# Loading half of x's rows through a second DMA queue in a LoRA kernel

## The reference

```python
B_sel = B[adapter_ids]          # (64, 16, 1024)
A_sel = A[adapter_ids]          # (64, 1024, 16)
Bx  = jnp.einsum('bni,bri->bnr', x, B_sel)
out = jnp.einsum('bnr,bor->bno', Bx, A_sel)
x = x + out                     # the scaling factor is 16 / 16 = 1
```

## Time and profile before

| | |
|---|---|
| median of 3 runs | 92.23 us |
| the profiled execution | 91.81 us |
| its span, first to last instruction | 90.0 us |
| mean granted TensorE clock | 0.982 |
| TensorE busy | 80.6 us, 90% |
| GpSimd, VectorE, ScalarE busy | 62.9, 59.7, 59.4 us |
| moved by DMA | 34.82 MB, mean 387 GB/s |
| of this in q1 (SyncE) and q10 (ScalarE) | 27.79 and 6.82 MB |

### The profile page before, as it was taken

One profiled execution on the slowest core, in us unless ns is written; L12 is line 12 of the kernel. 1 busy time (PEld: TensorE's weight loads), 2 busy tenths in 40 slices (PEclk: granted clock), 3 DMA queues, 4 the chain that ended last, 5 costly groups with the idle time before them and its releaser, 6 DMA issues.

```text
span 90.0 us, 3579 instructions
## 1 busy us (share of the span) xinstructions
PE 80.6 (90%) x1451; PEld 60.7 (67%) x1451; DVE 59.7 (66%) x111; ACT 59.4 (66%) x154; POOL 62.9 (70%) x141
## 2 busy tenths in 40 slices
PE   3995999999999999999999999998999999989300
PEld 3974778768787878787777868685778686633100
DVE  0309968277777786859595959595939595999100
ACT  1429869959696969695959686877595868524200
POOL 6103992999999999979696979696859692900000
PEclk9999999999999999999999999999999999999975
DMA  1999999999999999999999999999999999997990
GB/s 29 325 412 422 410 408 408 402 415 413 399 409 404 410 409 400 400 415 413 419 422 413 417 419 410 415 426 406 419 417 415 417 413 400 404 391 306 408 395 36
DMA packets 9249, 34.82 MB, mean 387 GB/s; under 512 B 402, under 2 KB 914, under 8 KB 9234
## 3 DMA queue, kind: packets, MB, share of 16 engines
q1 hardware_dynamic: 7520, 27.79, 77.2%
q10 hardware_dynamic: 1714, 6.82, 18.8%
HBM read 17.83 MB, written 16.78 MB: 384 GB/s over the span
## 4 chain that ended last, share of the span: by engine, by line
PE 83%; DMA 6%; ACT 4%; issue 1%
PE t_bank L255 35%; PE bx_bank L268 21%; PE y_banks L288 18%; DMA x_all<-in_A 6%; PE y_banks L315 2%; PE t_bank L319 2%; ACT x_all L365 1%; PE bx_bank L319 1%; PE y_banks L242 1%; ACT b_table L369 1%; PE bx_bank L315 1%; ACT x_all L424 1%; ACT x_t L377 1%; PE t_bank L315 1%; PE bx_bank L242 0%
## 5 line engine op out<-in xcount | busy, mean ns | idle before, releaser
L465 DVE TENSOR_TENSOR x_all<-y_banks,x_all 128x1024 f32<-128x1024 f32 x29 | 35.5, 1224 | 15.5 <-PE y_banks L288 15.1
L377 ACT COPY x_t<-t_bank 128x512 f32<-128x512 f32 x64 | 34.4, 590 | 13.7 <-PE t_bank L255 12.8
L198 POOL CAST a_duo<-a_table 128x512 fp32r x64 | 36.6, 615 | 3.7 <-PE y_banks L288 2.1
L255 PE MATMUL t_bank<-ident,x_all 128*128 128x128 f32 x256 | 35.0, 280 | 1.2 <-DMA x_all<-in_x 0.8
L255 PEld LDWEIGHTS t_bank<-ident,x_all 128*128 128x128 f32 x256 | 27.4, 141 | 8.4 <-issue 5.2
L188 POOL COPY b_duo<-b_table 128x256 f32 x64 | 22.9, 401 | 5.8 <-PE bx_bank L268 5.8
L268 PE MATMUL bx_bank<-x_t,b_duo 128*32 128x64 f32 x1024 | 20.8, 222 | 0.0
L268 PEld LDWEIGHTS bx_bank<-x_t,b_duo 128*32 128x32 f32 x1024 | 15.7, 109 | 5.5 <-issue 5.5
L288 PE MATMUL y_banks<-a_duo,bx_parts 64*128 64x512 f32 x112 | 17.3, 421 | 0.3 <-issue 0.3
L456 DVE TENSOR_TENSOR bx_parts<-bx_bank,bx_parts 32x64 fp32r<-32x64 f32 x64 | 14.1, 220 | 1.5 <-ACT bx_parts L392 0.4
L392 ACT CAST bx_parts<-bx_bank 32x64 fp32r<-32x64 f32 x64 | 13.0, 204 | 1.9 <-PE bx_bank L268 1.3
(11 more groups left out here) (31 smaller groups left out, 21.2 us busy)
## 6 DMA issues: line engine op xcount, KB each, us to landing
x_all<-in_x SPq DMA_DIRECT2D x3, 3072.0 KB, 30.7
out_y<-x_all ACTq DMA_DIRECT2D x2, 3072.0 KB, 17.8
x_all<-in_x SPq DMA_DIRECT2D x3, 1024.0 KB, 12.4
out_y<-x_all SPq DMA_DIRECT2D x1, 3072.0 KB, 14.5
out_y<-x_all SPq DMA_DIRECT2D x6, 512.0 KB, 4.7
x_all<-in_x SPq DMA_DIRECT2D x4, 512.0 KB, 7.2
x_all<-in_x SPq DMA_DIRECT2D x1, 2048.0 KB, 20.0
out_y<-x_all SPq DMA_DIRECT2D x1, 2048.0 KB, 10.4
```

What stands on the lines that cost most here:

```text
L198: last = nc.gpsimd.tensor_copy(a_duo[duo % 2][:, k, :], a_table[:, bass.ds(adapters[k] * BANK, BANK)])
L255: last = nc.tensor.transpose(t_bank[unit % 2][:, c * P:(c + 1) * P], x_all[:, 2 * duo + tile, at:at + P], ident[:, :])
L377: nc.scalar.copy(x_t[duo % 2][:, half * HALF:(half + 1) * HALF, tile, :], t_bank[unit % 2][:, :].rearrange("p (c n) -> p c n", c=HALF)).th ...
L465: nc.vector.tensor_tensor(here, product, here, ALU.add).then_inc(y_drained, 1)
```

## The change

The first eight loads, tiles 0 to 15, are each cut into two transfers of 64 rows: SyncE loads the even rows, ScalarE the odd ones, into the same tiles, and both count up the same semaphore, for which TensorE then waits to 32. ScalarE issues the odd rows of the first six loads (tiles 0 to 7) right behind B and the ids, those of the seventh (tiles 8 to 11) in duo 0, and those of the eighth (tiles 12 to 15) in duo 2. The cuts of the loads behind tile 8 change too.

```diff
-    LOADS = [(t, t + 1) for t in range(4)] + [(t, t + 2) for t in range(4, 10, 2)]
-    LOADS += [(10, 14)] + [(t, t + 6) for t in range(14, TILES, 6)]
+    LOADS = [(t, t + 1) for t in range(4)] + [(4, 6), (6, 8), (8, 12), (12, 16)]
+    SHARED = len(LOADS)
+    LOADS += [(16, 20), (20, 26), (26, TILES)]
+    SHARED_AT_START = 6
+    SHARED_IN_DUO = {0: 6, 2: 7}
...
-                sp.dma_start(x_all[:, first:end, :], rows[:, first:end, :]).then_inc(x_loaded[n], 16)
+                own = slice(0, P, 2) if n < SHARED else slice(0, P)
+                sp.dma_start(x_all[own, first:end, :], rows[own, first:end, :]).then_inc(x_loaded[n], 16)
...
-                    pe.wait_ge(x_loaded[load], 16)
+                    pe.wait_ge(x_loaded[load], 32 if load < SHARED else 16)
...
             act.dma_start(id_row[:, :], ids.rearrange("(o s) -> o s", o=1)).then_inc(ids_loaded, 16)
 
+            def load_odd_rows(n):
+                first, end = LOADS[n]
+                own = slice(1, P, 2)
+                act.dma_start(x_all[own, first:end, :], rows[own, first:end, :]).then_inc(x_loaded[n], 16)
+
+            for n in range(SHARED_AT_START):
+                load_odd_rows(n)
...
+                if duo in SHARED_IN_DUO and duo:
+                    load_odd_rows(SHARED_IN_DUO[duo])
                 if duo + 1 < DUOS:
                     copy_x(duo + 1, 0)
                     copy_x(duo + 1, 1)
                 if duo == 0:
                     copy_a(A_BY_ACT[1])
+                    load_odd_rows(SHARED_IN_DUO[duo])
```

## The result

The changed kernel took 93.02 us (median of 20 runs) where the kernel before took 92.18 beside it: the ratio is 1.0088 [1.0071, 1.0105], slower by 0.8 us or 0.9%. The forecast was 95.1 us with a range from 93.9, so the direction was right and the size, 2.9 us, more than three times too large. What both show alike is taken as the effect of the change, what one alone shows is not.

The account below looks back on a forecast made before the run. TensorE and the DMA engines were both read as full, with no slack behind TensorE's chain from A's landing. Only A's 2.9 us delay counted, other terms 0 or hidden: 92.23 + 2.9 = 95.1 us, range 93.9 to 98.9.

Parts of the forecast that it names:

- (1): Start, queues q1 and q10: odd rows directly behind B keep slowing A's 1 KB packets, so A lands 2.9 us late.
- the prediction's own signs of being wrong: The prediction called itself wrong if A still lands near 6 us, or if the time between TensorE's duos grows.
- (2): TensorE's start: x's even rows stand behind A, tile 0 lands at about 10.2 us, start 2.9 late, no second wait.
- (3): ScalarE's start: six issues, 3.1 to 3.4 us, before its table load, hidden behind A; otherwise 0.25 to 0.45 us.
- (4): ScalarE in duos 0 and 2: two later issues of 0.4 to 0.6 us fit into existing waits; price 0.
- (5): SyncE's queue: eleven loads as before, eight half as long; long issues and changed cuts hold up nobody; 0.
- (6): TensorE's wait for 32 is counted in (2); at the end the DMA engines have room for the last stores, so 0.
- A not held up: Rival at the start: odd rows move only after A, which lands at 6.06; 0.3 us faster at best, 91.9; chance 0.08.
- a smaller delay: Case at the start: A gets more than every second turn, half the delay, 1.45 us, 93.7 (92.6 to 94.4); chance 0.08.
- The clock: Rival at TensorE's start: idling 3.7 us lowers the clock, adding 0.6 to 1.6 us, taken 1.0: 96.1 us; chance 0.17.
- not held up behind it: Rival in ScalarE's issue of tiles 8 to 11: SyncE's full queue stalls it, 6.6 us, 101.7; chance 0.04.
- Half-row transfers are slower: Rival in x's loads: 64-row transfers run below 410 GB/s, rate 0.9 costing 2.3 us; taken as 97.5; chance 0.21.

Follow-up runs that it names:

- ids_first: The changed kernel with ScalarE's first two issues exchanged, the ids ahead of B; 92.73 us, 1.0077 against the kernel before.
- ids_second: The changed kernel with the ids issued behind tile 0's odd rows; 93.1 us, 1.0101 against the kernel before.
- a_rows: The changed kernel with A loaded in 4 KB rows, 128 pieces in place of 512, making the A table wrong; 92.58 us, 1.0074 against the kernel before.
- tile0_whole: The changed kernel with tile 0 loaded whole by SyncE, ScalarE issuing five halves at the start; 92.36 us, 1.0024 against the kernel before.
- late_share: The changed kernel with halves only from tile 4 on, tiles 0 to 3 whole by SyncE; 92.97 us, 1.0101 against the kernel before.
- after_again: The changed kernel run once more without edit, for a second trace; 93.08 us, 1.0077 against the kernel before.
- pe_late_3: The kernel before with the first unit's transposes done eight times, 28 more, 3.05 us, no transfer changed; 93.17 us, 1.0094.
- one_queue: The changed kernel with both halves of every shared load issued by SyncE, one behind the other; 92.37 us, 1.0026 against the kernel before.
- pe_late_1b: The kernel before with the first unit's transposes done four times, 12 more, 1.3 us, run again for a trace; 92.44 us, 1.0023.

## Why the prediction was wrong, point by point

**(1), the step that failed.** It said that the odd rows "are queued before q10 runs dry", and so "A keeps its 4 KB neighbour until its own end". They were issued in time, but a transfer issued is not yet one that moves: their first packet came 4.25 us after the issue, 1.56 after B's end, and A landed at 5.91 instead of 8.9, the first of the prediction's own signs of being wrong. The term, 2.9 us for A, measured 0. Five more kernels show 3.8 to 4.4 us (ids_first, ids_second, a_rows, tile0_whole, late_share), also with the ids elsewhere and with a quarter of A's packets. (B's last packet was at 4.77 and A's at 5.61 in the kernel before, not at "about 4.2" and 5.2; the forecast does not hang on either.) The 73 to 74 of the earlier trace rows was read rightly, and is 79 to 78 in the changed kernel, while both queues send; what was missing is whether both would. The row that could have told it was in the trace of before: ScalarE's first store, and the queues in the 3.5 us from its issue.

```profile
35.56 0.41 ACTq L403 DMA_DIRECT2D out_y<-x_all  x1
...
q1 hardware_dynamic: 352, 1.40, 101.4%
```

From 35.6 to 39.1 us SyncE's queue did 352 packets and q10 not one; its first came at 39.20, 3.6 us after the issue. I used B's start instead, which came 1.6 us after its issue, when only A's first packets were moving. But some 4 us is no rule either. The changed kernel's first store by SyncE, issued at 60.02 us onto an empty queue, has its first packet at 60.96, after 0.94 us, though ScalarE's queue filled the engines all that time:

```profile
q10 hardware_dynamic: 95, 0.39, 100.5%
q1 hardware_dynamic: 1, 0.00, 1.1%
```

The same store in the kernel before, issued at 57.01, waited 3.5 us. So the wait was there at the start of every kernel that was traced with a second queue, and what sets its length is open. The Trainium skill (DMA: Bandwidth & Descriptors, Specifications) gives about 0.6 us to the first byte of a transfer that SyncE or ScalarE issues. The runs here show 0.8 us at the least (a store late in after_again, the engines nearly idle), 1.1 us (A), 1.6 us (B), and 0.9 to 4.4 us beside a busy queue; the measurement decides.

**(2), right in its form, with another cause and size.** The start of TensorE was to move with tile 0, by 2.9 us; it moved by 1.61, since it is tile 0's odd half, and not A, that is late. That no second wait is added at tile 1 held (1.59 there). Leaving tile 0 whole took back about 0.6 of the 0.84 us, together with one of ScalarE's issues.

**(3), mis-sized.** Six issues were put at 3.1 to 3.4 us from SyncE's median of 495 ns; they took 4.12 us (623 ns at the median of all eight). Since A did not move, they were no longer hidden behind it: the cast of A came 1.24 us late. This lies beneath the first delay (ScalarE's table copies end at 9.43, and its copy of x at 9.67 waits for TensorE), so it cost little of its own here; where tile 0 came in time it was next, as ids_first and ids_second show: 0.88 and 1.38 us at tile 1, not the 0.25 to 0.45 that the prediction gave for this case.

**(4), (5), right.** The two later issues took 0.61 us each and held no one, the cuts cost nothing (1.0008).

**(6), "The end: 0", the second step that failed**, and with it the sentence "There is no slack behind to take it up". I took TensorE's busy share for the bound of the end and read the chain of waits as a proof. The kernel before had 1.4 us of slack there by the traces, about 2 by pe_late_3: its last store landed 4.8 us after the issue, because a few DMA engines were behind the others. A start late by 1.6 us, grown to 2.08 at the last copy in after_again, less 1.45 given back, is 0.63; the median spans say 0.6, and the rest of the 0.84 lies around the span. The two errors add: had the start really been 2.9 us late, the end would have moved by about 0.9, as pe_late_3 shows with 3.05.

**The rivals.** "A not held up" was right in its premise and wrong in what follows: A landed on time and the kernel was slower nevertheless, because I let x's odd rows flow at once. That 93.02 falls into the band of "a smaller delay" (92.6 to 94.4) is chance: A was not delayed at all. The clock stayed at 1.00 over a gap in TensorE's work from 7.31 to 8.98, 1.67 us; the gap of 3.7 us that the rival needed did not come, so it is untested rather than out. Its 421 ns for the warm-ups were taken at a granted clock that reads 1.00 from 2 to 4 us, so they said nothing of the clock. ScalarE's issue at 19.40 took 0.61 us though SyncE's queue was full and its issue lasted from 13.69 to 27.3: not held up behind it. "Half-row transfers are slower" is a small effect, 0.2 us in one_queue, not 2.3 or more (and its price for a rate of 0.9 left out the 0.6 us that its price for 0.75 took off). The Trainium skill (SBUF — State Buffer, The DMA setup-cost knee) advises all 128 partitions for transfers that bound a kernel; the 289 and 307 GB/s in two stretches of half rows agree with it, the 413 and 416 in the others show that it matters little here.

## What to carry to other kernels

Before moving a transfer to a second queue, find in the trace what an issue onto that queue takes to its first packet while the first queue is busy (here 3.8 to 4.4 us at the start), count what the issues cost the engine that makes them, and never put half of the first thing needed there. Two queues share by packets, not by need, so work wanted late takes its turn from work wanted now. A busy TensorE does not prove that it sets the end: compare the time from its last work to the end of the span with that in a run where TensorE is certainly late (here 5.85 and 4.4 us), and the difference is slack.

## What was not expected of the hardware

- From issue to first packet: 0.8 to 1.6 us on quiet engines, 3.6 to 4.4 us for ScalarE's loads and first store beside SyncE's queue, but 0.9 to 3.5 us for SyncE's first store beside ScalarE's. The wait does not follow the transfers ahead of it on its own queue. Where it is spent is not settled.
- The last 512 KB store lands 3.4 us after its issue when all DMA engines end together, 4.8 in the kernel before, where a few engines end up to 1.4 us behind the others.
- ScalarE's issues took 623 ns at the median while SyncE was issuing as well, against 495 for SyncE's in the kernel before.
- 12 transposes more (1.3 us) at the start made TensorE's last work 2.07 us late in pe_late_1b; one wait behind tile 5 adds 0.84, and later ones, in this trace or in that of the kernel before, cancel.
- Kernels with six odd-row issues at the start have 0.4 to 0.6 us more around their span in some executions (five of 20 of the changed kernel); with five issues (tile0_whole) or two (late_share) none of 18 has. Why is open.
